# Edge attention of a graph layer on one core: a wider scrap clear behind every gather, and gathers held by the ring alone

## The reference

```python
src = K_h[src_idx]
dest = Q_h[dst_idx]
score = src * dest / jnp.sqrt(jnp.asarray(D, x.dtype))
score = score * E
score = jnp.exp(jnp.clip(score.sum(-1, keepdims=True), -5.0, 5.0))
msg = V_h[src_idx] * score
wV = jax.ops.segment_sum(msg, dst_idx, num_segments=N)
Z = jax.ops.segment_sum(score, dst_idx, num_segments=N)
h_out = wV / (Z + 1e-06)
```

## Time and profile before

| what | value |
|---|---|
| median of two runs | 1071.3 us |
| span of the profiled execution | 1231.7 us |
| GpSimd busy in it | 919.8 us (75%), 1572 instructions |
| TensorE busy in it | 824.3 us (67%) |
| VectorE busy | 595.7 us (48%) |
| ScalarE busy | 457.8 us (37%) |
| gathers from `kv_table` | 750, mean 952 ns |
| gathers from `x` | 32 |
| clears of `spacer` | 782, mean 221 ns |

### The profile page before, as it was taken

How to read it: one execution, slowest core, us unless ns; L and a number is a source line. 1 busy time by engine, 2 the same in 40 slices (tenths; PEclk the granted TensorE clock), 3 DMA queues, 4 the chain that set the end, 5 groups by cost and what they waited for, 6 DMA issues and landing times.

```text
span 1231.7 us, 13818 instructions
## 1 busy us (share of the span) xinstructions
PE 824.3 (67%) x3375; PEld 455.9 (37%) x3375; DVE 595.7 (48%) x1583; ACT 457.8 (37%) x1094; POOL 919.8 (75%) x1572
## 2 busy tenths in 40 slices
PE   6518565986676666667676667666767676776763
PEld 4415232543343333333333334333333333333433
DVE  5104344954444464445444545445554545454645
ACT  3206232743343343333333334333434343433331
POOL 8882777167878778778787787887777877877783
PEclk9757787988877888887888787887878877878885
DMA  9922344454545445445444444444444444444321
GB/s 245 277 77 77 104 126 109 137 145 120 144 116 138 125 112 131 125 111 127 122 121 125 108 135 117 120 132 120 111 130 125 128 127 112 121 130 126 92 77 51
DMA packets 124525, 153.29 MB, mean 124 GB/s; under 512 B 57885, under 2 KB 92191, under 8 KB 124436
## 3 DMA queue, kind: packets, MB, share of 16 engines
q0 software_dynamic: 37008, 75.28, 23.9%
q1 hardware_dynamic: 80608, 73.74, 21.7%
q10 hardware_dynamic: 6822, 3.31, 1.0%
HBM read 142.26 MB, written 9.98 MB: 124 GB/s over the span
## 4 chain that ended last, share of the span: by engine, by line
POOL 37%; PE 22%; issue 16%; another core or an unknown queue 10%; DVE 6%; DMA 6%; ACT 2%; SPq 0%; DVEq 0%; POOLq 0%
POOL kv L493 30%; POOL spacer L500 7%; DMA kv<-kv_table,src_idx 5%; PE ps_eq L1030 4%; PE ps_eq L1023 4%; PE ps_qe_seg L1055 3%; PE ps_last L1055 3%; PE ps_eq_qe L1023 2%; PE ps_qe_seg L1041 2%; PE ps_eq_qe L1030 1%; PE ps_eq_qe L1041 1%; DVE ps_last L768 1%; DVE node_stage L743 1%; DMA w_all<-biases_in 1%
## 5 line engine op out<-in xcount | busy, mean ns | idle before, releaser
L493 POOL DMA_INDIRECT kv<-kv_table,src_idx x750 | 714.2, 952 | 285.5 <-issue 114.7
L602 ACT ACTIVATE ps_last<-clipped 128x32 f32<-128x32 f32 x196 | 39.4, 201 | 542.4 <-issue 397.2
L1030 PE MATMUL ps_eq<-pick_t,q_win 128*96 128x512 f32 (+1 forms) x262 | 169.5, 735 | 78.7 <-ACT e_t L597 58.4
L761 DVE TENSOR_TENSOR kq<-kv,ps_qe_seg 128x384 f32<-128x384 f32 x98 | 53.9, 550 | 260.7 <-DMA kv<-kv_table,src_idx 195.7
L1023 PE MATMUL ps_eq<-ea,w_all 128*96 128x512 f32 (+1 forms) x262 | 172.5, 747 | 8.1 <-issue 7.4
L500 POOL MEMSET spacer<- 128x128 f32 x782 | 172.8, 221 | 2.7 <-remote 2.2
L761 DVE TENSOR_TENSOR kq<-kv,ps_eq_qe 128x384 f32<-128x384 f32 x98 | 54.1, 552 | 238.3 <-DMA kv<-kv_table,src_idx 175.5
L1055 PE MATMUL ps_qe_seg<-node_stage 128*104 128x80 f32 x784 | 116.2, 306 | 54.5 <-issue 28.9
L1055 PE MATMUL ps_last<-node_stage 128*104 128x80 f32 x780 | 108.2, 292 | 49.3 <-issue 24.2
L588 ACT ACTIVATE distance<-rel_bc,neg_part 80x512 bf16<-80x512 bf16 x196 | 138.4, 706 | 1.8 <-issue 0.6
L1055 PEld LDWEIGHTS ps_qe_seg<-node_stage 128*104 128x104 f32 x784 | 105.2, 218 | 64.6 <-issue 49.6
(11 more groups left out here) (90 smaller groups left out, 788.2 us busy)
## 6 DMA issues: line engine op xcount, KB each, us to landing
ea<-ea_t_in SPq DMA_DIRECT2D x196, 192.0 KB
rel_bc<-rel_rows_dram SPq DMA_DIRECT2D x196, 80.0 KB
kv<-kv_table,src_idx POOLq DMA_INDIRECT x750
q_win<-q_table SPq DMA_DIRECT2D x196, 30.0 KB
kv_table<-node_stage SPq DMA_DIRECT2D x5, 576.0 KB
x_both<-x_t_in SPq DMA_DIRECT2D x5, 480.0 KB, 8.9
x_both<-x_rows_in ACTq DMA_DIRECT2D x10, 240.0 KB
out<-node_stage SPq DMA_DIRECT2D x11, 192.0 KB
```

Of the source, the lines that this page charges most:

```text
L493: pool.indirect_dma_start(rows[0:n, :], None, table, bass.IndirectOffsetOnAxis(ap=src_idx[0:n, tile:tile + 1], axis=0)).then_inc(semaphore ...
L761: nc.vector.tensor_tensor(kq[:, group % 2, 0:n, :], kv[:, slot, 0:n, 0:DIM], ps_qe[group % 2][:, 0:n * DIM].rearrange("p (t d) -> p t d", ...
L1030: nc.tensor.matmul(ps_eq[(2 * group + 1) % 3][0:DIM, 0:n], q_win[:, slot, :], pick_t[:, group % 3, 0:n], start=True, stop=True).then_inc(e ...
```

## The change

The scrap tile becomes 128x256, so that each of the 782 clears writes 256 columns. The waits of groups 32 and up are taken out, and the wait of the ring (`e_msg`, the group 16 earlier) holds for all groups from 16 on.

```diff
-PACED_FROM = 32
...
-    assert KV_RING > 2 * SUMMED and PACED_FROM >= KV_RING
+    assert KV_RING > 2 * SUMMED
...
-        spacer = sb("spacer", [P, 128], F32)
+        spacer = sb("spacer", [P, 256], F32)
...
             def windowed(streamed):
                 for group in range(EARLY, GROUPS):
-                    slot, ahead = group % KV_RING, min(group + 2, GROUPS - 1)
-                    if KV_RING <= group < PACED_FROM:
+                    slot = group % KV_RING
+                    if group >= KV_RING:
                         pool.wait_ge(e_msg, group - KV_RING + 1)
                     for t in range(tiles_of(group)):
-                        if group >= PACED_FROM:
-                            pool.wait_ge(*((e_seg, group - 3), (e_e, ahead + 1), (e_q, ahead + 1), (e_turn, group + 1))[t])
                         gather(kv[:, slot, t, :], kv_table, group, t, e_kv[slot])
                         space(group * GROUP_TILES + t)
```

## The result

The changed kernel took 1154.05 us (1153.76 and 1154.34), against 1071.3 before: ratio 1.077, 95% interval 1.074 to 1.080.

What follows compares the result with a forecast made beforehand. The prediction took GpSimd's serial gathers and clears to bound the kernel from first gather to last. 1071.3 us plus 86 for 782 wider clears, minus 0 for removed waits, gave 1157 us, range 1115 to 1185.

Steps and rivals of the forecast that it cites:

- The sum: Whole kernel: 1071.3 us plus 86 for wider clears, minus 0 for waits taken out, gives 1157 us.
- The lower slope: GpSimd's clears: index fills of 512 against 1 column give 0.83 ns a column, 107 ns for 128 more.
- the one of 1.8: GpSimd's clears: the reference page's 1.8 cycles an element for a tight loop, 192 ns a clear, 150 us, 1221 us total.
- the clear is serial: GpSimd between gathers: a longer clear delays the next gather by its whole growth, so all 782 clears pay in full.
- No waits in a timed run: GpSimd, first to last gather: about 5 us of waiting in the timed kernel before; removing waits counted as 0.
- The floor worked out for the span: Changed kernel's profiled span if GpSimd never waits: 4.6 + 782 x 1.447 + 16.4 = 1152.6 us.
- The floor of before: Kernel before if GpSimd never waits: 4.6 + 782 x 1.337 + 16.4 = 1066.5 us.
- nearly all these waits exist only in the profiled execution: GpSimd's roughly 157 us of profiled waits: said to be absent from timed runs, which take 160 us less.
- Readers fall back: Without pacing, late wakes fill the ring at 7.0 us a group over 164 groups, 1342 us; chance 6%, mild form 4%.
- The waits were real: From group 32 on, pacing costs timed runs too: up to 120 us back, 1037 us; chance 6%.
- The other two rivals: GpSimd's clears: extra width hidden or short-cut, 1071 us, 4%; or costing up to 221 ns more each, 1244 us, 5%.
- What the profile of after should show: Clears about 0.33 us, gather starts 1.44 to 1.46 apart, no GpSimd wait for TensorE, no 35 us stop at group 32.

Runs made afterwards that it cites:

- e1: Clear widened to 256 columns alone, waits of groups 32 and up kept, against the kernel before: 1190.7 us, ratio 0.978.
- e12: Against e2, message sums take only a group's last tile, one matmul of four: 1268.6 us, ratio 1.029 to the kernel before.
- e2: Changed kernel with the clear back at 128 columns, so only the waits of groups 32 and up taken out: 1283.8 us, ratio 1.055 to the kernel before.
- e4: Changed kernel with a clear of one column instead of 256, still without the waits: 1337.5 us, ratio 1.099 to the kernel before.
- e11: Against e2, gathers of groups 8 and up fetch 96 floats instead of 192, half the bytes: 1303.4 us, ratio 1.058 to the kernel before.
- e5: The changed kernel, unchanged, run again beside the kernel before on another chip: 1200.1 us, ratio 0.988 to the kernel before.
- e7: Changed kernel with clears moved: none behind a group's first three gathers, four of 256 columns behind the fourth: 1187.8 us, ratio 0.978 to the kernel before.
- e3: The kernel before, unchanged, run again for a second profile: 1219.1 us, ratio 1.000.
- e8: Kernel before with a clear of one column instead of 128, its waits kept: 1232.7 us, ratio 1.015.

## Why the prediction was right, and where it was not

**The sum: right, 1157 against 1154.** The one term was the clear: 110 ns taken, 107 measured (328 - 221), 83.7 us instead of 86. The lower slope, from the index fill of 512 columns, hit it exactly; the rule of 1.03 cycles an element of the Trainium skill's GPSIMD Engine Reference, section "Performance versus the Vector engine", came to 110 and the trace agrees with 107, and the one of 1.8 (150 us) does not hold for this clear. That the clear is serial holds: all of its growth is in the distance between gathers, 1.44 us in the timeline.

**No waits in a timed run: right for the recorded pair.** The floor worked out for the span was 1152.6, the span is 1152.5, and GpSimd's gathers from the table waited 0.2 us for others. That the two agree to 0.1 us is in part luck: between the first and the last gather lie 781 steps and not 782, 1.4 us too much in the sum, and head and tail came out 1.0 us longer (4.77 and 17.2). The floor of before, 1066.5, is too high by 1.3 us for the same reason. That the waits of the kernel before gave nothing back was derived from its median and the floor; 1071.3 + 83.7 = 1155.0 leaves about 1 us for them. In the prompt condition the two edits were not run apart, so it remains an inference there.

**What failed: "nearly all these waits exist only in the profiled execution".** Late wakes are in the trace of every kernel of e1 to e12, each of them one of the timed executions, and not in that of the recorded changed kernel. What I took for the price of profiling is a condition in which a kernel runs or does not. The floor argument that I drew from it was still sound, because it rested only on 1071.3 us being so close to 1066.5; but it held for that condition alone. The word "timed" in each step should have read "in the condition of the two timed runs". The trace of before had a clue: its floor was a property of the program, its late wakes were not, and a difference of 160 us between a profile and a median is no usual price, as 1.8 us of after and 1.77 to 1.95 of the later runs show, each between a time and its own span.

**The rivals.** "Readers fall back" was given 6%, and its place and its form were right: in the late condition, with the ring alone, they do. Its price was too high: I took 7.0 us a group from the earlier trace rows, 1342 us; in e2 the keys' multiply of groups 8 and 176 starts at

```profile
151.07 0.54 DVE L758 TENSOR_TENSOR kq<-kv,ps_eq_qe 128x384 f32<-128x384 f32 x1
...
1187.59 0.54 DVE L758 TENSOR_TENSOR kq<-kv,ps_eq_qe 128x384 f32<-128x384 f32 x1
```

6.2 us a group, and the run takes 1284. It did not decide because the pair was prompt, and in the late condition the wide clear takes most of it away. "The waits were real" is wrong in both: in the prompt condition by the sum above, and in the late one taking them out made the kernel slower with either clear (1217 to 1284, 1191 to 1200). The other two rivals are refuted by the 107 ns.

**What the profile of after should show.** Clears of 0.33, starts 1.44 to 1.46 apart, no wait for TensorE, the stop at group 32 gone: all there. Wrong was that the keys' multiply would no longer wait for gathers. It waits 502 us for them, since readers at 2.6 us a group use up the ring (at group 20 the multiply starts at 130.5, 3.2 us behind the group's last gather) and are then on GpSimd's heels, paced or not:

```profile
DVE kq L758 <- DMA kv<-kv_table,src_idx: 502.2, 168, 5.3
```

## What to carry to other kernels

Where one engine works serially, its first start, count times step, and its tail give a floor; if the median stands on the floor, whatever lengthens the step is paid in full and whatever removes waits gives nothing. But ask that the profile and the median come from the same condition: if they differ by more than a few microseconds, time the kernel again, and compare versions only beside each other on one chip, because here the same change was 8% slower in one condition and 1.2% faster in the other. And a piece of useless work on a busy engine can act as a throttle, as the wide clear does here; before taking it for waste, or for cost, run both settings in each condition. Then ask in which stretch the gain lies: what looks like a better steady pace (e1) was all in the start.

## What the runs showed of the hardware

In the late condition waits for TensorE's semaphores end up to 16 us late while GpSimd issues gathers (e4 and e11, ScalarE's copy). Two other kinds of wait do not: ScalarE's exponential starts 0.03 to 0.04 us (median over the groups) after the later of VectorE's clip and its own instruction before, in the profile of before as in e2 and e12, and where ScalarE's copy is what VectorE's product waits for, that starts 0.03 us after it (median); but the copy, which waits for TensorE, was late 83 times in e2. With the ring alone the late wakes are many where GpSimd, when nothing holds it, takes up to 5.8 us for four gathers (e5), evenly spaced or in lumps, and few where it takes 5.96 (e7); with pacing, which brings the mean to 5.8 us, they are few behind group 32 too (12.3 us of the copy's waits in e3, 4.6 in e1, 25.3 in e8, against 337.5 in e5); halving the gathers' bytes or taking three of four summing matmuls away does little. What makes a run late or prompt, whether the chip or something else about the execution, and what TensorE's semaphores and the gathers share, stays open: no run of a kernel in both conditions on one chip is at hand, and a run with fewer gather descriptors in the same time was not tried.
